# Attention in five rounds of rows a unit, with products in three runs and four rows turned by VectorE

## The chip, the cores and the metric

The kernel runs on one core of a Trainium2 chip. The metric is the device time of one execution in microseconds, as the median of three runs. The engines are TensorE (PE in the profile, PEld for its weight loads), VectorE (DVE), ScalarE (ACT), GpSimd (POOL) and SyncE (SP), which issues most of the DMAs.

## The reference

The input x has shape (8, 1024, 256), float32. One layer norm feeds two branches, and the output is x plus both.

```
xn  = layernorm(x)
qkv = einsum('bse,ehd->bshd', xn, w_qkv)        # 16 heads, q, k, v of 64 each
att = einsum('bshd,hde->bse', attention(q, k, v), w_out)   # causal, logits / sqrt(64), softmax over keys
ffn = top-2-of-8 mixture of experts on xn, capacity 2048 tokens an expert, hidden 1024, relu
out = x + att + ffn
```

## The kernel before, in words

The kernel first does layer norm and routing, then the experts (`experts`), which write their results y to DRAM, and then `attention_and_sum`, the function that the change touches. Products that need precision are made of three matmuls of a high and a low part each (qh and ql, kh and kl, oh and ol, and so on): ScalarE copies a bank of PSUM into the high tile, and VectorE subtracts that from the bank into the low tile.

Attention goes by units: one pair of heads (h = 0, 1) of one batch, UNITS = 8 x 8 = 64. A unit has queries in eight rows of 128 (i = 0 to 7); with the causal mask row i has (i+1) x 128 keys. A unit runs in 16 steps, and each engine's program walks all steps of all units in the same written order, with semaphores between engines; nothing is scheduled at run time. Two steps make one row:

- `scores`: TensorE fills S[0] and S[1] (two banks each) with the row's scores of both heads. It waits until VectorE has read the row before (`negmax`).
- `row_max`: VectorE adds the mask (`late`), writes the scores to a tile pr and gives their minimum, since the scores are negated.
- `softmax`: ScalarE makes the exponential in place with its sum. `reciprocals`: VectorE. The scale by it: GpSimd, in place in pr.
- The scaled row has to be turned, so that keys lie on partitions. For rows 0 to 5 TensorE does it six steps later (`turn_p`, LAG = 6), in blocks of 128 x 128 into the banks T[0] and T[1], chunks of up to four blocks, and `keep` copies each chunk to pT on VectorE (ten chunks a unit) or ScalarE (six). For rows 6 and 7 VectorE transposes squares of 32 x 32 (`square`) into the tile squares, and 16 DMA strips, 12 issued by SP (`place`) and 4 by GpSimd (`place_last`), put the squares in their places of pT. The last unit turns all its rows on TensorE.
- `values`: products of the turned rows with v, by groups of two rows (g = 0 to 3, with 2, 4, 6 and 8 key blocks), into one bank O of 256 columns. `group`: ScalarE copies O to oh, VectorE makes ol.

Between these stand the pieces, each at a step of its own (`STEP_OF`) and in a work bank (`BANK_OF`; two of the three banks are the upper halves of S): p0 to p3 project q and k of the next unit (halves f = 0, 1; p0 and p2 are q, p1 and p3 are k), v0 and v1 project v of the next two units, xn turns a tile of normalised input, and o0 to o3 multiply a group with w_out and add to the residual `res` on VectorE. A piece waits until the piece before it in its bank has been read.

GpSimd also has, at steps of `POOL_AT`: `split_w` and `split_wv` (weights into high and low parts), `choose`, two `fetch`es (gathers of y by indirect DMA), `weigh`, which waits for both fetches, `add` and `total`, which adds the experts' result to `res`. All stand in one queue with the scales.

Of the kernel before, what the change touches and what calls it, by code (L numbers as in the profile page):

```python
# [845 lines left out]
def attention_and_sum(nc, k, x, xn_dram, w_qkv, w_out, pick, y_dram, out, start):  # L846
# [4 lines left out]
    STEPS, LAG, RING = 2 * QT, 6, 8  # L851
# [4 lines left out]
    PART = 8  # L856
    PARTS = [-(-(2 * g + 2) // PART) for g in range(GROUPS)]
    AHEAD = Start.TILES
    VW = 4 * HDIM
    width = lambda s: (s // 2 + 1) * P  # L860
    shift = lambda s: P if width(s) == HALF + P else 0
    slot = lambda n, s: (n * STEPS + s) % RING

    WIDE = STEPS - STEPS // GROUPS
    BL = 32
    QUARTERS = P // BL
    CH = [[b for b in (min(HT, s // 2 + 1), s // 2 + 1 - HT) if b > 0] for s in range(STEPS)]  # L870
    FIRST_CH = [sum(len(x) for x in CH[:s]) for s in range(STEPS + 1)]
    CHUNKS = FIRST_CH[WIDE]
    assert all(FIRST_CH[4 * g] % 2 == 0 for g in range(GROUPS))
    KEPT_BY_ACT = {1, 10, 11, 12, 14, 15} | set(range(CHUNKS, FIRST_CH[STEPS], 2))
    KEPT_BY_DVE = set(range(FIRST_CH[STEPS])) - KEPT_BY_ACT
    in_squares = lambda n, s: s >= WIDE and 0 <= n < UNITS - 1
    by_pe = lambda n, s: 0 <= n < UNITS and not in_squares(n, s)
# [7 lines left out]
    NEXT = 1  # L885
    done_in = lambda n, g: n + (g >= NEXT)
    SHORT = 2 * HT
    BEFORE = ["p0", "p1", "p2", "p3", "v0", "v1"]
    BY_ACT = {"p0", "p1", "p2", "p3", "xn", "v0", "v1"}
    BY_DVE = {"p0", "p1", "p2", "p3", "xn", "o0", "o1", "o2", "o3"}  # L890


    POOL_AT = {'place0': 0, 'place1': 5, 'fetch0': 2, 'fetch1': 5, 'weigh': 6, 'add': 7, 'total': 14, 'split_w': 13, 'split_wv': 10}

    def pieces(n):
        if n < 0:
            return BEFORE
        there = {"p": n + 1 < UNITS, "x": n + AHEAD < TILES, "v": n + 1 < UNITS}

        return [p for p in STEP_OF if there.get(p[0], n < UNITS if p[0] == "o" and int(p[1]) < NEXT else n > 0)]  # L900

    class Pieces:
        def __init__(self, sem_, own):
            self.sem, self.value, at = sem_, {}, 0
            for n in range(-1, UNITS + 1):
                for p in pieces(n):
                    at += p in own
                    self.value[n, p] = at
# [5 lines left out]
    with ExitStack() as c:  # L914
# [6 lines left out]
        qh, ql, kh, kl = (two(lambda i: sb(f"{n}{i}", [P, SEQ], F32R)) for n in ("qh", "ql", "kh", "kl"))  # L921
        vv = two(lambda i: sb(f"vv{i}", [P, QT, VW]))

        pT_even, pT_odd = (sb(f"pT{g}", [P, 2, QT - 2 + 2 * g, GQ]) for g in range(2))
        pT = [[t[:, h] for t in (pT_even, pT_odd)] for h in range(2)]

        wide = pT_odd[:].rearrange("p h k q -> p (h k q)").rearrange("p (a x r) -> p a x r", x=4, a=QUARTERS)

        sq = sb("squares", [P, QUARTERS, 4, QT, BL])
        pr = start.pr + [sb(f"pr{i}", [P, SEQ]) for i in range(len(start.pr), RING)]  # L930
        negm, rsum, rinv = (sb(n, [P, RING]) for n in ("negm", "rsum", "rinv"))
        late = start.late
        oh, ol = (two(lambda i: sb(f"o{n}{i}", [P, GQ], F32R)) for n in "hl")
# [28 lines left out]
        with ExitStack() as pre:  # L962
# [4 lines left out]
            bank = [T[0], T[1], W0, S[0]]  # L967
# [41 lines left out]
        kept = two(lambda i: Count(sem(f"s_kept{i}"), CHUNKS // 2))
        squared = Count(sem("s_squared"), STEPS - WIDE)  # L1010
        placed = Count(sem("s_placed"), 16 * QUARTERS * (QUARTERS - 1))
        last_placed = Count(sem("s_last_placed"), 16 * QUARTERS)
        pv = Count(sem("s_pv"), GROUPS)
        ohi, olo = Count(sem("s_ohi"), GROUPS), Count(sem("s_olo"), GROUPS)
        filled = Pieces(sem("s_filled"), set(BANK_OF))
        act = Pieces(sem("s_act"), BY_ACT)
        dve = Pieces(sem("s_dve"), BY_DVE)

# [12 lines left out]


        lagged = lambda n, s: (n, s - LAG) if s >= LAG else (n - 1, s - LAG + STEPS)
        SQUARE_LAG = 4
        squaring = lambda n, s: (n, s - SQUARE_LAG) if s >= SQUARE_LAG else (n - 1, s - SQUARE_LAG + STEPS)


        AFTER = [13, 14, 19, 27]

        def group_at(n, s):  # L1040

            for d in range(2):
                for g in range(GROUPS):
                    part = s + d * STEPS - AFTER[g]
                    if 0 <= part < PARTS[g] and 0 <= n - d < UNITS:
                        return n - d, g, part
            return None


        OH_LATER, OL_LATER = 0, 0  # L1050
        before = lambda n, s, d: (n, s - d) if s >= d else (n - 1, s - d + STEPS)

        ALL = [(n, s) for n in range(UNITS) for s in range(STEPS)]
        END = [(UNITS, s) for s in range(16)]

        def strip(a, b):

            to, of = slice(b * BL, (b + 1) * BL), slice(a * BL, (a + 1) * BL)
            return wide[to, a].rearrange("p x r -> p (x r)"), sq[of, b].rearrange("p x k i -> p (x k i)")

        @block.sync
        def _(e):
# [8 lines left out]
            def place(n):  # L1071
                e.wait_ge(squared.sem, squared.at(n, STEPS - WIDE))
                e.wait_ge(pv.sem, pv.at(n, GROUPS - 2))
                for a in range(QUARTERS - 1):
                    for b in range(QUARTERS):
                        e.dma_start(*strip(a, b)).then_inc(placed.sem, 16)  # L1076

            def store(b, g):
                e.wait_ge(dve.sem, dve.at(done_in(b * PAIRS + PAIRS - 1, g), f"o{g}"))
                e.dma_start(outv[:, b, 2 * g:2 * g + 2], res[:, 2 * g:2 * g + 2]).then_inc(stored[g].sem, 16)  # L1080
# [8 lines left out]
            e.wait_ge(wlo.sem, wlo.at(0, MC))  # L1089
            load_w(2)  # L1090
            for n in range(UNITS):
                if n + AHEAD < TILES:
# [3 lines left out]
                b, u = n // PAIRS, n % PAIRS  # L1096
                if n == 0:
                    e.wait_ge(s_wolo, 1)
                    for g in range(GROUPS):
                        refill(0, g)  # L1100
                if b > 0 and u == 0:
                    refill(b, 0)
                if b > 0 and u == 1:
                    refill(b, 3)
                if n > 0:
                    place(n - 1)
                if b > 0 and u == 0:
                    store(b - 1, 1)
                    refill(b, 1)
                    store(b - 1, 2)  # L1110
                if n + 3 < UNITS:
                    e.wait_ge(wlo.sem, wlo.at(n + 1, MC))
                    load_w(n + 3)
# [3 lines left out]
                if b > 0 and u == 0:  # L1117
                    store(b - 1, 3)
                    refill(b, 2)
                if u == PAIRS - 1:  # L1120
                    store(b, 0)
            for g in range(NEXT, GROUPS):
# [434 lines left out]
```

## Time and profile before

| | |
|---|---|
| median of three runs | 3163.03 us (3161.75 to 3163.10) |
| span of the profiled execution | 3160.1 us |
| TensorE matmul busy | 3031.1 us, 96% |
| TensorE weight loads busy | 2408.4 us, 76% |
| VectorE busy | 2185.9 us, 69% |
| ScalarE busy | 1711.1 us, 54% |
| GpSimd busy | 1604.3 us, 51% |

The span runs from the first to the last instruction of the profiled execution. Busy time is the time in which an engine has an instruction under way. Matmuls overlap, so TensorE's busy time is not a measure of full speed. The attention takes the last 2250 us or so of the span.

### The profile page before, as it was taken

Reading aid. Unit: us, or ns where it says so; the run is one execution under the profiler, and the core shown is the slowest. Engines: PE = TensorE matmul, PEld = TensorE weight load, DVE = VectorE, ACT = ScalarE, POOL = GpSimd, SP = SyncE. Lnnn points to the kernel's source line nnn. Section 1 sums busy time; section 2 is a strip of 40 time slices with the busy share of each in tenths; the row PEclk is TensorE's granted clock in tenths of the full one; section 3 lists DMA queues with packets and bytes.
Section 4 is the critical chain, followed back from the end, with each engine's and each line's share of the span. In section 5 each row is a group of like instructions: output and inputs, shape, how many; then the busy total and the mean of one; then the engine's idle time right before and its main releaser. Section 6 shows DMA issues by size and latency. Waiting matters only on the chain.

```text
span 3160.1 us, 64379 instructions
## 1 busy us (share of the span) xinstructions
PE 3031.1 (96%) x22707; PEld 2408.4 (76%) x22707; DVE 2185.9 (69%) x5088; ACT 1711.1 (54%) x3866; POOL 1604.3 (51%) x2378
## 2 busy tenths in 40 slices
PE   4699999999989999999999999999999999999998
PEld 3589998999977777777777777777777777777776
DVE  7744443444347778777877787787778877877876
ACT  3454444445446555555555555555555555555554
POOL 3122221222126666666666666666666666666664
PEclk8799999999999999999999999999999999999999
DMA  7112222122113333343333333333442343334222
GB/s 240 49 48 72 77 73 69 47 76 79 51 57 83 95 84 101 80 103 92 87 89 95 101 79 92 102 86 83 101 105 75 86 107 91 82 89 112 71 72 71
DMA packets 204437, 272.64 MB, mean 86 GB/s; under 512 B 61265, under 2 KB 161617, under 8 KB 204129
## 3 DMA queue, kind: packets, MB, share of 16 engines
q1 hardware_dynamic: 179712, 201.94, 23.8%
q0 software_dynamic: 24416, 66.65, 8.0%
q8 instruction: 187, 3.06, 0.4%
q14 instruction: 122, 0.99, 0.1%
HBM read 102.80 MB, written 33.55 MB: 43 GB/s over the span
## 4 chain that ended last, share of the span: by engine, by line
PE 61%; ACT 5%; issue 4%; DVE 1%; SPq 0%; DMA 0%; DVEq 0%; ACTq 0%
PE S L1221 15%; PE O L1258 13%; PE T L1234 10%; PE W L1137 9%; PE S L1137 3%; ACT pr L1296 3%; PE W L1152 3%; PE S L1152 3%; PE W L1172 3%; PE S L1172 2%; ACT pT L1288 1%; PE S L1160 0%; DVE pr L1352 0%; ACT oh L1320 0%; SPq L1076 0%
## 5 line engine op out<-in xcount | busy, mean ns | idle before, releaser
L1296 ACT ACTIVATE pr<-pr,negm 128x128 f32<-128x128 f32 (+7 forms) x1024 | 787.3, 770 | 669.4 <-DVE negm L1352 669.4
L1497 POOL TENSOR_SCALAR pr<-pr,rinv 128x128 f32<-128x128 f32 (+7 forms) x1024 | 755.8, 745 | 424.9 <-DVE rinv L1358 422.5
L1352 DVE CUSTOM_DVE_ANT_0 pr<-S,late 128x128 f32<-128x128 f32 (+7 forms) x1024 | 730.4, 750 | 38.1 <-PE S L1221 22.3
L1258 PE MATMUL O<-pT,vv 128*64 128x256 f32 (+1 forms) x5120 | 556.2, 364 | 3.5 <-DMA pT<-squares 3.1
L1258 PEld LDWEIGHTS O<-pT,vv 128*64 128x64 f32 x5120 | 346.1, 137 | 205.3 <-issue 45.4
L1234 PE MATMUL T<-ident,pr 128*128 128x128 f32 x2718 | 423.4, 281 | 32.5 <-DVE pT L1288 17.8
L832 DVE TENSOR_TENSOR hl<-h,hh 128x512 fp32r<-128x512 f32 x256 | 191.1, 747 | 316.2 <-ACT hh L793 316.0
L1288 DVE COPY pT<-T 128x512 f32<-128x512 f32 (+3 forms) x644 | 305.2, 499 | 142.2 <-PE O L1258 111.9
L1234 PEld LDWEIGHTS T<-ident,pr 128*128 128x128 f32 x2718 | 296.8, 140 | 138.9 <-issue 118.9
L789 ACT ACTIVATE h<-pH,b1c 128x512 f32<-128x512 f32 x256 | 176.1, 688 | 365.6 <-PE pH L719 338.8
L1221 PE MATMUL S<-kh,qh 64*128 64x512 f32 (+2 forms) x1536 | 316.8, 408 | 6.5 <-DVE negm L1352 6.5
L731 PE MATMUL pY<-w2h,hh 128*128 128x256 f32 x1024 | 287.8, 281 | 2.5 <-DVE hl L832 2.5
L731 PE MATMUL pY<-w2l,hh 128*128 128x256 f32 x1024 | 289.1, 282 | 0.0
L731 PE MATMUL pY<-w2h,hl 128*128 128x256 f32 x1024 | 288.0, 281 | 0.0
L1392 DVE STREAM_TRANSPOSE squares<-pr 128x896 f32<-128x896 f32 x252 | 287.7, 1161 | 0.0
L1458 POOL DMA_DIRECT2D pT<-squares x252 | 136.2, 544 | 260.0 <-DVE squares L1392 249.9
L1221 PE MATMUL S<-kh,ql 64*128 64x512 f32 (+2 forms) x1536 | 264.1, 338 | 0.0
L1221 PE MATMUL S<-kl,qh 64*128 64x512 f32 (+2 forms) x1536 | 263.3, 338 | 0.0
L1221 PEld LDWEIGHTS S<-kh,qh 64*128 64x128 f32 x1536 | 144.0, 183 | 126.2 <-issue 65.8
L719 PE MATMUL pH<-xh,w1h 128*128 128x512 f32 x512 | 205.3, 401 | 4.2 <-DVE xl L804 2.6
L719 PE MATMUL pH<-xh,w1l 128*128 128x512 f32 x512 | 201.5, 394 | 0.0
L719 PE MATMUL pH<-xl,w1h 128*128 128x512 f32 x512 | 201.4, 393 | 0.0
(194 smaller groups left out, 6391.3 us busy)
## 6 DMA issues: line engine op xcount, KB each, us to landing
pT<-squares SPq DMA_DIRECT2D x756, 128.0 KB
pT<-squares POOLq DMA_DIRECT2D x252, 128.0 KB, 3.8
y<-yb SPq DMA_DIRECT2D x128, 128.0 KB, 1.7
wr<-in_L_attn_w_qkv SPq DMA_DIRECT2D x128, 128.0 KB, 2.3
x<-in_L_attn_x SPq DMA_DIRECT2D x16, 512.0 KB, 9.7
xn<-xn SPq DMA_DIRECT2D x16, 512.0 KB, 4.5
w1r<-in_L_ffn_w SPq DMA_DIRECT2D x8, 1024.0 KB, 5.0
w2r<-in_L_ffn_w SPq DMA_DIRECT2D x8, 1024.0 KB, 8.0
```

The lines of the kernel that those rows point to most:

```text
L719: ins = e.matmul(pH[hc % 4][:], w[par][:, m, ws], xx[q][:, m, :], start=(n == 0), stop=(n == 3 * MC - 1))
L731: ins = e.matmul(pY[t % 2][:], hs[q][:, hc, ts_], ws[par][:, hc, :], start=(hc == 0 and n == 0), stop=(hc == HC - 1 and n == 2))
L832: e.tensor_tensor(hl[q][:, hc, :], h32[hc % 2][:], hh[q][:, hc, :].bitcast(F32), ALU.subtract).then_inc(hlo.sem, 1)
L1137: ins = e.matmul(W, ws[:, 2 * m + of_k], xs[:, t0:t0 + HT, m, :], start=(i == 0), stop=(i == 3 * MC - 1))
L1221: ins = e.matmul(S[h][:, a:b], t[q][hs, i * P:(i + 1) * P], u[q][hs, a - off:b - off], start=(j == 0), stop=(j == len(terms) - 1))
L1234: ins = e.transpose(T[ch % 2][:, b * P:(b + 1) * P], pr[slot(n, s)][:, kt * P:(kt + 1) * P], k["ident"][:])
L1258: ins = e.matmul(O[hs, a:GQ], vv[n // 2 % 2][:, kt, vs], turned_p, start=(kt == 0), stop=(kt == KT - 1))
L1288: ins = e.activation(dst, src, ACT.Copy) if own is KEPT_BY_ACT else e.tensor_copy(dst, src)
L1296: e.activation(pr[i][:, 0:w], pr[i][:, 0:w], ACT.Exp, bias=negm[:, i:i + 1], scale=-1.0, accum_out=rsum[:, i:i + 1]).then_inc(expd.sem, 1)
L1352: e.tensor_tensor_reduce(pr[i][:, 0:w], S[s % 2][:, off:off + w], late[:, SEQ - w:], 1.0, -MASKED, ALU.add, ALU.min, negm[:, i:i + 1]).the ...
L1392: e.transpose(sq[:, :, x % 2 * 2 + x // 2, 0:KT, :], pr[slot(n, s)][:, 0:KT * P].rearrange("p (k b i) -> p b k i", b=QUARTERS, i=BL)).then ...
L1497: e.tensor_scalar(pr[i][:, 0:width(s)], pr[i][:, 0:width(s)], rinv[:, i:i + 1], 1.0, ALU.mult, ALU.mult).then_inc(scaled.sem, 1)
```

## The change

The unit is rearranged. It has five rounds of four steps, and a round holds one or two rows: (3, 2), (4, 1), (5, 0), (6), (7). The rows of a round stand side by side in S (`OFFSET`), whose four banks now belong to scores alone. TensorE makes all scores of a round, then VectorE takes all minima, and the scores of the next round wait for the last of them. Row 4 is multiplied at 768 columns.

Rows 4 to 7 are turned by VectorE's squares, and groups 2 and 3 each have 16 strips, which SP and GpSimd place at two times of the unit. Rows 0 to 3 are turned by TensorE in six turns (t30 to t11), which are pieces with steps and banks like the others and are all copied by ScalarE. Products come in three runs, groups 0 and 1 together, then 2, then 3, with O and oh, ol of 512 columns, and each group has a pT of its own. q has one buffer (no longer two), and so has the second half of k; for that p2 and p3 project q and k of the unit itself at its steps 0 and 1, and the scores of the round (4, 1) wait for p3's low part. There are three work banks apart from S, and none named T. On VectorE and ScalarE a piece's work stands one step behind the step where TensorE fills it.

```diff
+    ROUNDS = [(3, 2), (4, 1), (5, 0), (6,), (7,)]
+    SUB, RING = 4, 3
+    STEPS = SUB * len(ROUNDS)
+    OFFSET = {3: 0, 2: HALF, 4: 0, 1: HALF + 2 * P, 5: 0, 0: HALF + 2 * P, 6: 0, 7: 0}
+    multiplied_width = {0: 2 * P, 4: 6 * P}
+    SQUARED = [4, 5, 6, 7]
+    TURNS = {"t30": [(3, 0, 0, 4)], "t31": [(3, 1, 0, 4)], "t20": [(2, 0, 0, 3)], "t21": [(2, 1, 0, 3)],
+             "t10": [(1, 0, 0, 2), (0, 0, 0, 1)], "t11": [(1, 1, 0, 2), (0, 1, 0, 1)]}
...
-    STEP_OF = {'v0': 0, 'p0': 2, 'o1': 4, 'o2': 5, 'xn': 5, 'p1': 6, 'v1': 6, 'p2': 7, 'p3': 9, 'o3': 12, 'o0': 14}
-    BANK_OF = {'p0': 2, 'p1': 0, 'p2': 2, 'p3': 2, 'o2': 2, 'xn': 0, 'v0': 2, 'o3': 2, 'v1': 1, 'o0': 2, 'o1': 1}
+    STEP_OF = {"p2": 0, "p3": 1, "o0": 2,
+               "o1": 4, "v0": 5,
+               "t30": 8, "t31": 8, "o2": 9, "t20": 10, "t21": 10,
+               "v1": 12, "p0": 13, "t10": 14, "t11": 14,
+               "p1": 16, "o3": 17, "xn": 18}
+    BANK_OF = {"p2": 0, "p3": 1, "o0": 2,
+               "o1": 0, "v0": 1,
+               "t30": 2, "t31": 0, "o2": 1, "t20": 2, "t21": 0,
+               "v1": 1, "p0": 2, "t10": 0, "t11": 1,
+               "p1": 0, "o3": 2, "xn": 1}
...
-    POOL_AT = {'place0': 0, 'place1': 5, 'fetch0': 2, 'fetch1': 5, 'weigh': 6, 'add': 7, 'total': 14, 'split_w': 13, 'split_wv': 10}
+    RUN_STEP = [(0, 19), (1, 7), (1, 15)]
+    RUN_GROUPS = [(0, 1), (2,), (3,)]
+    POOL_AT = {"choose": 1, "place3_0": 4, "place3_1": 5, "split_w": 6, "fetch0": 8, "fetch1": 9, "weigh": 11, "add": 12,
+               "split_wv": 14, "place2_0": 16, "place2_1": 17, "total": 19}
...
+            def scores(n, r):
+                if r == 0:
                     e.wait_ge(dve.sem, dve.at(n - 1, "p1"))
+                if r == 1:
+                    e.wait_ge(dve.sem, dve.at(n, "p3"))
+                if (n, r) > (0, 0):
+                    e.wait_ge(negmax.sem, negmax.at(n, FIRST[r]))
...
+            def turn_p(n, name):
+                W, unit, at = work_bank(name), min(n, UNITS - 1), 0
+                i, h, _, _ = TURNS[name][-1]
+                e.wait_ge(scaled.sem, scaled.at(unit, PLACE[i, h] + 1))
...
```

The minima on VectorE wait for the room's last reader three rounds before, and for the scores of the whole round:

```diff
+            def row_min(n, j):
+                i, h = ORDER[j]
+                r, off, w, c0 = ROUND_OF[i], OFFSET[i], width(i), column(n, i, h)
...
+                e.wait_ge(score.sem, score.at(n, FIRST[r + 1] - 1 + h))
+                e.tensor_tensor_reduce(room_of(n, i, h)[:, off:off + w], S[h][:, off:off + w], late[:, SEQ - w:], 1.0, -MASKED,
+                                       ALU.add, ALU.min, negm[:, c0:c0 + 1]).then_inc(negmax.sem, 1)
```

The new order of the engines' programs, in turn TensorE, ScalarE, VectorE and GpSimd (whose other work of a step stands behind the step's scale). `names_at` gives the pieces of a step, `run_at` the run of products, `back(n, s, d)` is d steps earlier:

```diff
+                if n < UNITS and s % SUB == 0:
+                    scores(n, s // SUB)
+                for name in names_at(n, s):
+                    work(n, name)
+                if run_at(n, s):
+                    values(*run_at(n, s))
...
+                if run_at(*back(n, s, 1)):
+                    run(*run_at(*back(n, s, 1)))
+                for name in names_at(*back(n, s, 1)):
+                    if by_act(name):
+                        work(back(n, s, 1)[0], name)
+                r, x = s // SUB, s % SUB
+                if n < UNITS and FIRST[r] + x < FIRST[r + 1]:
+                    softmax(n, FIRST[r] + x)
...
+                r, x = s // SUB, s % SUB
+                if run_at(*back(n, s, 1)):
+                    run(*run_at(*back(n, s, 1)))
+                if n < UNITS and x < len(ROUNDS[r]):
                     for h in range(2):
+                        row_min(n, FIRST[r] + 2 * x + h)
...
+                if n < UNITS and 2 <= x < 2 + len(ROUNDS[r]):
+                    reciprocals(n, ROUNDS[r][x - 2])
+                for name in names_at(*back(n, s, 1)):
+                    if by_dve(name):
+                        work(back(n, s, 1)[0], name)
+                m, q = back(n, s, SUB)[0], (r - 1) % len(ROUNDS)
+                if x >= 2 and 0 <= m < UNITS and in_squares(m, ROUNDS[q][0]):
+                    square(m, ROUNDS[q][0], x - 2)
...
+                if x >= 2:
+                    scale(n, FIRST[r] + x - 2)
+                elif m >= 0 and len(ROUNDS[q]) > 1:
+                    scale(m, FIRST[q] + 2 + x)
```

## Rows read from the trace of the kernel before

**Rows 1.** windows, steady stretch: busy us (and instructions) by engine, clock, DMA share, GB/s

```profile
1348.00:1696.00 348.00, 343.17 (x2681) 259.53 (x2680) 274.09 (x670) 200.29 (x491) 217.53 (x335) 1.00 0.36 90
```

**Rows 2.** chain of waits in order of time, one unit: start us, us, what

```profile
2030.07 0.14 issue
...
2031.05 1.42 PE W L1152 x12
...
2035.26 2.53 PE O L1258 x24
...
2047.65 1.48 PE W L1137 x6
...
2049.13 1.25 PE S L1221 x12
...
2051.18 3.39 PE O L1258 x32
...
2056.00 0.59 PE T L1234 x4
...
2058.53 1.59 PE S L1221 x12
```

**Rows 3.** timeline of VectorE (DVE), one unit: start us, us, line, operation

```profile
2026.75 1.22 DVE L1352 CUSTOM_DVE_ANT_0 pr<-S,late 128x1024 f32<-128x1024 f32 x1
...
2031.43 2.09 DVE L1392 STREAM_TRANSPOSE squares<-pr 128x896 f32<-128x896 f32 x2
...
2033.81 0.42 DVE L1352 CUSTOM_DVE_ANT_0 pr<-S,late 128x256 f32<-128x256 f32 x1 [0.24 <-PE S L1221]
...
2046.65 0.69 DVE L1383 TENSOR_TENSOR ql<-W,qh 128x512 fp32r<-128x512 f32 x1 [1.80 <-ACT qh L1311]
...
2047.33 0.80 DVE L1352 CUSTOM_DVE_ANT_0 pr<-S,late 128x640 f32<-128x640 f32 x1
...
2048.06 0.82 DVE L1352 CUSTOM_DVE_ANT_0 pr<-S,late 128x640 f32<-128x640 f32 x1
...
L1288 DVE COPY pT<-T 128x512 f32<-128x512 f32 (+3 forms) x644 | 305.2, 499 | 142.2 <-PE O L1258 111.9
```

**Rows 4.** timeline of GpSimd (POOL): second fetch of y and the weighing behind it

```profile
1035.23 1.02 POOL L1471 DMA_INDIRECT yg<-y,sel  x1 [0.30 <-issue]
...
2044.36 1.02 POOL L1471 DMA_INDIRECT yg<-y,sel  x1 [0.30 <-issue]
...
2049.56 0.93 POOL L1477 TENSOR_SCALAR yg<-yg,sel 128x256 f32<-128x256 f32 x2 [1.34 <-DMA yg<-y,sel]
...
2429.91 1.02 POOL L1471 DMA_INDIRECT yg<-y,sel  x1 [0.30 <-issue]
...
2433.39 0.93 POOL L1477 TENSOR_SCALAR yg<-yg,sel 128x256 f32<-128x256 f32 x2 [1.72 <-DMA yg<-y,sel]
```

**Rows 5.** timeline of ScalarE (ACT): exponentials and a copy

```profile
2028.02 1.14 ACT L1296 ACTIVATE pr<-pr,negm 128x1024 f32<-128x1024 f32 x1
...
2049.01 0.82 ACT L1296 ACTIVATE pr<-pr,negm 128x640 f32<-128x640 f32 x1
...
2049.82 0.57 ACT L1311 ACTIVATE kh<-W 128x512 fp32r<-128x512 f32 x1
```

**Rows 6.** timeline of GpSimd: splits, scales and strip issues of one unit

```profile
2027.77 0.41 POOL L1433 TENSOR_SCALAR wr<-wr 128x256 f32<-128x256 f32 x1
...
2030.52 1.13 POOL L1497 TENSOR_SCALAR pr<-pr,rinv 128x1024 f32<-128x1024 f32 x1
...
2042.98 1.07 POOL L1458 DMA_DIRECT2D pT<-squares  x2
...
2051.83 1.56 POOL L1497 TENSOR_SCALAR pr<-pr,rinv 128x640 f32<-128x640 f32 x2
```

**Rows 7.** timeline of SP, and the page's DMA issues (KB each, us to landing)

```profile
2037.80 9.14 SPq L1076 DMA_DIRECT2D pT<-squares  x12
...
pT<-squares POOLq DMA_DIRECT2D x252, 128.0 KB, 3.8
```

More of the change, by code:

```diff
@@ new lines, in attention_and_sum @@
+    PLACE = {row: j for j, row in enumerate(ORDER)}
+    FIRST = [sum(2 * len(rows) for rows in ROUNDS[:r]) for r in range(len(ROUNDS) + 1)]
+    ROUND_OF = {i: r for r, rows in enumerate(ROUNDS) for i in rows}
+    OFFSET = {3: 0, 2: HALF, 4: 0, 1: HALF + 2 * P, 5: 0, 0: HALF + 2 * P, 6: 0, 7: 0}
+    width = lambda i: (i + 1) * P
+    multiplied_width = {0: 2 * P, 4: 6 * P}
+    room = lambda n, i: (len(ROUNDS) * n + ROUND_OF[i]) % RING
+    column = lambda n, i, h: 4 * room(n, i) + 2 * ROUNDS[ROUND_OF[i]].index(i) + h
@@ new lines, in attention_and_sum, with run_at @@
+    BEFORE = ["p0", "p1", "v0", "v1"]
+    by_act = lambda name: name[0] in "pvx" or (name[0] == "t" and not (len(name) == 4 and name[2] == "1"))
+    by_dve = lambda name: name[0] in "pox" or not by_act(name)
+    RUN_STEP = [(0, 19), (1, 7), (1, 15)]
+    RUN_GROUPS = [(0, 1), (2,), (3,)]
+    RUN_OF = {g: j for j, groups in enumerate(RUN_GROUPS) for g in groups}
+    RUNS = len(RUN_GROUPS)
+    def run_at(n, s):
+        for j, (later, step) in enumerate(RUN_STEP):
+            if s == step and 0 <= n - later < UNITS:
+                return n - later, j
+        return None
@@ L900, in pieces @@
-        return [p for p in STEP_OF if there.get(p[0], n < UNITS if p[0] == "o" and int(p[1]) < NEXT else n > 0)]
+            return [(0, p) for p in BEFORE]
+        there = {"p0": n + 1 < UNITS, "p1": n + 1 < UNITS, "p2": n < UNITS, "p3": n < UNITS, "v0": n + 1 < UNITS,
+                 "v1": n + 1 < UNITS, "xn": n + AHEAD < TILES}
+        own = [(s, p) for p, s in STEP_OF.items() if there.get(p, n > 0 if p[0] == "o" else n < UNITS)]
+        own += [(s, t) for (m, s), turns in END_TURNS.items() if m == n for t in turns]
@@ L902, in attention_and_sum @@
+        return sorted(own, key=lambda at: at[0])
     class Pieces:
@@ L905, in __init__ @@
             for n in range(-1, UNITS + 1):
-                for p in pieces(n):
-                    at += p in own
+                for _, p in pieces(n):
+                    at += own(p)
                     self.value[n, p] = at
@@ L1030, in attention_and_sum, with strip @@
         block = c.enter_context(nc.Block())
[L1033 to L1051, printed above, removed]
+        back = lambda n, s, d: (n, s - d) if s >= d else (n - 1, s - d + STEPS)
         ALL = [(n, s) for n in range(UNITS) for s in range(STEPS)]
-        END = [(UNITS, s) for s in range(16)]
-        def strip(a, b):
+        END = [(UNITS, s) for s in range(STEPS)]
+        names_at = lambda n, s: [p for at, p in pieces(n) if at == s] if n >= 0 else []
+        def strip(g, a, b):
             to, of = slice(b * BL, (b + 1) * BL), slice(a * BL, (a + 1) * BL)
-            return wide[to, a].rearrange("p x r -> p (x r)"), sq[of, b].rearrange("p x k i -> p (x k i)")
+            return wide[g][to, a].rearrange("p x r -> p (x r)"), sq[g][of, b].rearrange("p x k i -> p (x k i)")
         @block.sync
@@ L1118, in _ @@
                     store(b - 1, 3)
[L1119 to L1122, printed above, removed]
+                    refill(b, 3)
+            for g in range(GROUPS):
                 store(BATCH - 1, g)
@@ L1263, in _ @@
-            for name in BEFORE:
+                            vs = slice(n % 2 * P + h * HDIM, n % 2 * P + (h + 1) * HDIM)
+                            turned_p = wide_of(g, h, kt, a // P) if in_squares(n, 2 * g) else pT[g][:, h, kt, a:GQ]
+                            ins = e.matmul(O[hs, o0 + a:o0 + GQ], vv[n // 2 % 2][:, kt, vs], turned_p,
+                                           start=(kt == 0), stop=(kt == KT - 1))
+                ins.then_inc(pv.sem, 1)
+            for _, name in pieces(-1):
```

479 lines of the change are left out of this document (208 added, 271 removed).

## The prediction

> **What bounds the kernel now.** I read the page's totals first, then the windows, then the chain of waits in order of time, then the timelines of the single engines over one unit (one pair of heads of one batch; there are 64). In a 348 us window of the steady part TensorE is busy 343.2 us, VectorE 274, ScalarE 200, GpSimd 218, at a granted clock of 1.00 [rows 1]. A unit lasts 34.80 us: the second fetch of y of 29 units on starts 1009.13 us later [rows 4]. So TensorE is idle about 0.5 us a unit and works 34.3. The chain says the same: matmul pieces follow one another without a gap, scores, products, projections [rows 2]. What TensorE loses, a unit loses; that is true only while the others still fit under it.
>
> **What the change takes from TensorE.** Rows 4 and 5 of both heads were 2x(5+6) = 22 turned blocks. Four blocks take 0.59 us [rows 2], 0.148 each: 3.25 us go. Scores of row 4 grow from 640 to 768 columns. Scores of 768 columns took 1.25 and of 1024 took 1.59 [rows 2], 0.17 per 128 columns, so +0.17. TensorE's work after, from the pieces of rows 2: scores R1 (rows 3, 2) 1.62, R2 (4, 1) 1.80, R3 (5, 0) 1.80, R4 (6) 1.43, R5 (7) 1.59; four projections "p" of 1.5; two "v" of 1.42; four "o" of 0.75 (six matmuls of 256 columns, half of a "v", 0.71, and a little more behind a switch); xn 0.2; 20 blocks 2.96; products run A (groups 0, 1) 2.53, B 2.53, C 3.39. Sum 31.7 us. Group 2 is now read from squares, as group 3 was: 32 such matmuls took 3.39, 24 from plain tiles 2.53, the same 0.106 each, so that costs nothing. Were TensorE still never waiting, a unit would be 31.7.
>
> **What it adds elsewhere.** VectorE loses 10 copies of turned blocks a unit, 0.5 us each [rows 3], and gains four squares of 640 and 768 columns. Two squares of 896 take 2.09 [rows 3], 1.01 each; by columns 0.86 and 0.72, together +3.2. With 27.4 us a unit before [rows 1] it stays under 26, not the bound by its sum. ScalarE takes eight copies where it had six. GpSimd gets four more strip issues, two of which take 1.07 [rows 6], and SP twelve, where twelve take 9.1 [rows 7]: 18.3 of some 35 us, queued behind each other, R5's strips at one time of the unit and group 2's at another, so not the bound.
>
> **What it does to the order.** S now belongs to one round at a time, five rounds a unit, and the fillers between two rounds are few. The sum of shares can't tell whether they cover; I lay one unit out. Time 0 is the start of R5's scores. TensorE goes on 0.14 us after the copy it waited for [rows 2]; I give 0.2 us the other way, from TensorE's last matmul to VectorE's minimum, which waits for it [rows 3]. A minimum takes 0.73 at 640 columns (start to start) and about 0.14 less or more per 128 columns; a subtraction of 512 columns 0.61 and its result is there after 0.69 [rows 3]. An exponential takes 0.81 at 640, start to start, and 1.14 at 1024, about 0.11 per 128 columns, a copy 0.57, of which I count 0.5 where another instruction follows [rows 5]. A scale is 0.78 at 640 on GpSimd, 0.11 per 128 columns; the split of weights from 2027.77 to 2030.52 is 2.75 [rows 6].
>
> *First wait, R1 to R2.* TensorE: R5 scores to 1.6, p1 3.1, o3 3.85, xn 4.05, run A 6.55, R1 scores 8.2, p2 9.7, p3 11.2, o0 11.95, free. VectorE: minima of row 7 1.8 to 4.1; ScalarE's exponentials with p1's copy between them end at 5.95; behind the reciprocal that waits for them stand o3's addition, two squares of row 6 (2.0), xn's low part, run A's low part (0.6): 9.65. Only now come R1's four minima, though their scores were there at 8.4: 11.8. Then p2's low part, and p3's, which waits for ScalarE, where p3's copy stands behind two exponentials and p2's: 12.9; done 13.6. R2's scores wait for that by program: they start at 13.7. TensorE waits 1.75.
>
> *R2 to R3*: TensorE: scores 15.5, o1 16.25, v0 17.65, run B 20.2. VectorE: square of row 7 (1.17), a reciprocal, o0's addition (0.6), the other square: 16.6, also the moment from which group 3's strips can be issued; four minima (0.73 and 0.3, twice): 18.8, before TensorE is through. No wait.
>
> *Second wait, inside R3.* Scores end 22.0; t30, t31, o2 to 23.95. t20 wants t30's bank, and ScalarE copies t30 only after the exponential of row 5, whose minimum ends 1.15 after the scores (23.2): exponential 24.15, copy over at 24.7, t20 at 24.85, t21 likewise behind t31, done 25.75. TensorE has lost 0.85.
>
> *Third wait, inside R4.* TensorE: scores 27.2, v1 28.6, p0 30.1, t10, t11 to 31.0. t11 wants the bank of v1, whose copy stands behind row 6's exponential; VectorE is late at row 6's minimum: R3's minima are over at 24.4, but ScalarE's queue is exponential of 5, copies t30 and t31, exponential of 5 (26.2), one of 0, copies t20 and t21, one of 0 (27.9). So VectorE has the reciprocal of row 5 at 26.3, o2's addition and a square of row 4 to 27.6, the reciprocal of row 0 at 28.0, the other square to 28.7. Then minimum 29.8, exponential 30.85, v1's copy 31.45. t11 also wants row 0 scaled by GpSimd. That queue, from the squares of row 7 at 16.7: two strips 1.1, a scale 0.55, two strips 1.1, 0.76, split 2.75, 0.76, 0.45, fetch 1.1, 0.45, second fetch at 25.9. "weigh" stands before row 0's scale and waits for that fetch. In the usual unit it is there 5.2 us after its start, behind SP's strips; in a unit whose strips had just been issued, 3.5 [rows 4]. The new order has the fetch behind the last strip (16.7 + 9.1 = 25.8), so I take 3.5: 29.4, weigh 0.9, scale 0.35, add 0.73, scale 0.35: 31.8. t11 31.9 to 32.3, run C to 35.7, R5 again. Wait 1.3. Strips of group 3 have landed at 25.8 + 3.8 [rows 7] = 29.6, in time.
>
> 31.7 + 1.75 + 0.85 + 1.3 gives 35.6, the layout 35.7: 0.9 us more than 34.80. TensorE's removed work turned into three waits that are larger. Over 62 units +56 us. The first and last unit I take as before; the end may go either way by some 6 us.
>
> The Trainium skill (Perfetto Trace Analysis, Optimizing Scalar/DVE Operations) advises that where ScalarE and VectorE are not saturated but cause bubbles, cutting their instructions up may finish work sooner; this change groups them instead. By the shares alone a unit would be 31.7 us, by that rule bubbles should appear; no row of before shows it.
>
> The profiled execution spans 3160.1 us and the runs' median is 3163.0, so 2.9 us lie around it. 3163.0 + 56 = **3219 us**.
>
> **Rivals.**
> *A, GpSimd's fetch late.* If it takes the usual 5.2 us, it is there at 31.1: weigh to 32.0, scale 32.35, add 33.1, scale 33.45, t11 to 34.0, run C to 37.4, a period of 37.4 and +161 us, 3324. For it: this is the common case in the trace. Against: the strips are over earlier here. Chance 0.15.
> *B, faster: the first wait is shorter.* Place: VectorE's work between row 7's reciprocal and R1's first minimum. The layout has R1's minima 1.25 us behind their scores. The exact order of ends there is mine, and if VectorE is on time, with ScalarE's copies of p2 and p3 no later than TensorE fills them, R2 starts at 12.4 and all behind moves up: 34.4, 3163 - 25 = 3138. It decides from 0.9 us on. For it: 3.1 us of TensorE's work is really gone, so the waits must eat all of it. Against: the chain is a program order of seven instructions whose durations the trace shows. Chance 0.2.
> *C, all covered*: 31.7, 62 x -3.1, 2971. The second wait alone speaks against it, since the copy stands behind an exponential by program order. Chance 0.03.
> *D, about as before*: waits add up to 3.1. Chance 0.06.
> *Forecast*, three waits of 3.5 to 4.7 together, 3180 to 3260: 0.56.
>
> Within 0.2% (6 us) is no change that a measurement can tell. Faster: B and C, 0.23; same: D, 0.06; slower: the rest, 0.71. The forecast's own range is 3180 to 3260. The range of 8 in 10 reaches from 3120, most of B, to 3325, A.
>
> **What would show it.** A unit of 35 to 36.5 us between fetches; TensorE busy about 31.7 of it, some 89%; three gaps a unit: before R2's scores, released by VectorE's low part of k (1.7); before t20 and t21, by ScalarE's copies (0.9 together); before t10 or t11, by ScalarE's copy of v1 or GpSimd's scale (1.3). VectorE 26 us, GpSimd 24. Group 2's matmuls 0.106 us apart. Wrong would be: R1's minima start right behind their scores (B), weigh waits long behind the fetch and t11 for the scale (A), or run C waits for strips, which the layout excludes by 2.7 us.

## The result, and the profile after

The changed kernel takes 3289.95 us (median of four runs, 3280.67 to 3299.98) against 3162.39 before; the ratio is 1.0403, 95% interval 1.0382 to 1.0424. The forecast was 3219, with 3180 to 3260 as its own range and 3120 to 3325 as the range of 8 in 10. The way was right, but the loss of 127 us is more than twice the 56 that were forecast. It lies in the wide range only because that reached up to rival A, whose reason (a gather of 5.2 us) did not come about. Per unit the loss is 2.03 us and not 0.9: the second fetches of units lie 36.83 us apart on average over 60 units, against 34.80 [rows 4].

TensorE's totals on the page of the changed kernel:

```profile
PE 2915.4 (89%) x21321; PEld 2329.7 (71%) x21321; DVE 2120.5 (65%) x4640; ACT 1702.1 (52%) x3934; POOL 1740.3 (53%) x2631
```

The windows of the changed kernel, first the stretch of [rows 1], then two of 5 us (columns as there):

```profile
1348.00:1696.00 348.00, 304.88 (x2315) 232.16 (x2313) 248.12 (x570) 186.02 (x470) 226.87 (x358) 0.96 0.52 126
2010.00:2015.00 5.00, 5.00 (x35) 2.98 (x34) 1.80 (x3) 0.55 (x2) 3.76 (x6) 0.71 0.36 98
2030.00:2035.00 5.00, 5.00 (x32) 4.36 (x32) 4.39 (x12) 2.54 (x6) 3.56 (x7) 0.67 0.48 119
```

TensorE is busy 304.9 of 348 us (343.2 before), VectorE 248 (274.1 before), both less than before, and no engine is full. New is the clock: 0.96 over the stretch, and 0.71 and 0.67 in the two short windows, that is, 1.2 GHz for more than half of them and 2.4 GHz for the rest. Before it was 1.00 over the stretch. Both short windows come behind gaps of TensorE:

```profile
2008.79 0.52 PE L1183 MATMUL W<-ident,pr 128*128 128x128 f32 x3 [1.94 <-POOL pr L1429]
...
2028.67 0.50 PE L1225 MATMUL S<-khf,qh 64*128 64x512 f32 x2 [1.95 <-DVE kls L1383]
```

The chain of waits of the changed kernel, one unit from the low part of run A's products (start us, us, what):

```profile
2024.11 0.65 DVE ol L1399
2024.76 0.60 DVE pr L1349
2025.41 0.82 ACT pr L1287 x2
2026.22 0.48 ACT qh L1307
2026.70 0.70 ACT pr L1287 x2
2027.41 0.49 ACT khs L1307
2027.93 0.69 DVE kls L1383
2028.62 1.15 DVE squares L1392
...
2029.81 0.59 DVE res L1375
2030.40 1.16 DVE squares L1392
...
2031.85 1.05 POOL pT L1460 x2
...
2036.67 1.44 POOL wl L1441 x2
...
2039.52 1.06 POOL yg L1473
...
2041.30 4.39 DMA yg<-y,sel
...
2045.77 0.94 POOL yg L1479 x2
2046.71 0.35 POOL pr L1429
2047.06 0.70 POOL yg L1484
2047.75 0.36 POOL pr L1429
...
2048.25 0.52 PE W L1183 x3
2048.77 3.39 PE O L1257 x32
2052.16 1.64 PE S L1225 x11
```

In this stretch hardly any of it is TensorE up to t11. L1399 is ol, L1349 a minimum, L1287 an exponential, L1307 the copies of p2 and p3, L1383 p3's low part, L1392 the squares of row 7 with o0's addition (L1375) between them, L1460 GpSimd's strips, L1441 the split, L1473 the fetches, L1479 weigh, L1429 scales, L1484 add, L1183 t11, L1257 run C, L1225 the scores of round R5. It is the layout's path in its order. Against the start of the R5 scores before (2015.18 in the chain) the second fetch stands at 26.1, the layout had 25.9; the fetch takes 4.4 and the layout 3.5; from weigh to t11 it is 2.5, as laid out. Not every unit goes this way: of 49 units between 1200 and 3000 us the chain goes through the fetch in 34, and in 12 more it comes to t11 over ScalarE's copy of v1 instead.

TensorE's timeline in the changed kernel, with the idle time ahead of a row in brackets, and run C behind the last:

```profile
2047.20 0.52 PE L1183 MATMUL W<-ident,pr 128*128 128x128 f32 x3 [0.74 <-POOL pr L1429]
2048.25 0.52 PE L1183 MATMUL W<-ident,pr 128*128 128x128 f32 x3 [0.53 <-POOL pr L1429]
...
2065.66 0.49 PE L1225 MATMUL S<-khf,qh 64*128 64x512 f32 x2 [1.96 <-DVE kls L1383]
...
2076.48 1.03 PE L1183 MATMUL W<-ident,pr 128*128 128x128 f32 x6 [0.96 <-ACT pT L1277]
...
2083.49 0.52 PE L1183 MATMUL W<-ident,pr 128*128 128x128 f32 x3 [1.53 <-POOL pr L1429]
2084.54 0.87 PE L1183 MATMUL W<-ident,pr 128*128 128x128 f32 x3 [0.53 <-ACT qh L1307]
2085.34 4.73 PE L1257 MATMUL O<-pT,vv 128*64 128x256 f32 x32
```

The waits of 1900 us (51.5 units), in total, times and longest:

```profile
PE S L1225 <- DVE kls L1383: 99.8, 51, 2.0
...
PE W L1183 <- POOL pr L1429: 65.1, 72, 2.2
...
PE W L1183 <- ACT pT L1277: 50.4, 52, 1.0
...
PE W L1183 <- ACT vv L1298: 11.9, 16, 1.1
```

The three waits stand where they were forecast, the first 1.96 us (forecast 1.75), the second 0.96 (0.85), the third in two parts, 1.5 us a unit on average (1.3). The row at 2084.54 names the copy to qh, which t11 doesn't wait for by program; it ended about when row 0's second scale did, and that scale is what t11 waits for.

Before, the 32 matmuls of run C took 3.46 us as one piece of the timeline in all 58 units read:

```profile
2051.11 3.46 PE L1258 MATMUL O<-pT,vv 128*64 128x256 f32 x32
```

Here they take 4.73. Over 54 units of the changed kernel they average 3.98, in 19 of them more than 3.6, the longest 6.09: 0.52 us a unit that no step of the prediction had. In those 19 units t10 and t11 had waited 1.7 to 2.7 us together (2.28 on average), in the other 35 from 0.5 to 1.8 (1.05).

GpSimd's second fetch and the weighing behind it in the changed kernel answer to [rows 4]:

```profile
2041.30 1.04 POOL L1473 DMA_INDIRECT yg<-y,sel  x1 [0.19 <-issue]
...
2045.77 0.94 POOL L1479 TENSOR_SCALAR yg<-yg,sel 128x256 f32<-128x256 f32 x2 [1.33 <-DMA yg<-y,sel]
```

From start to weigh it is 4.47 us in this unit and 3.66 on average over 61 units (2.9 to 4.8). Before it was 5.2 on average over 64 units (3.5 to 6.1).

### The profile page after: what moved, and what is told of

It is laid out like the page before. It is cut to its first block, busy times and chain, and to the rows that moved or that the text cites. A ratio compares the mean times of both kernels' runs of the same rounds, so it can differ in the third digit from the quotient of the medians.

```text
span 3285.6 us, 61637 instructions
## 1 busy us (share of the span) xinstructions
PE 2915.4 (89%) x21321; PEld 2329.7 (71%) x21321; DVE 2120.5 (65%) x4640; ACT 1702.1 (52%) x3934; POOL 1740.3 (53%) x2631
## 4 chain that ended last, share of the span: by engine, by line
PE 18%; POOL 14%; DVE 14%; ACT 11%; issue 10%; DMA 5%; DVEq 0%; ACTq 0%; POOLq 0%
PE O L1257 9%; ACT pr L1287 8%; DVE squares L1392 6%; PE S L1225 6%; POOL pr L1429 5%; DMA yg<-y,sel 5%; POOL pT L1460 3%; DVE pr L1349 2%; DVE res L1375 2%; POOL wl L1441 2%; POOL yg L1473 1%; DVE kls L1383 1%; PE W L1183 1%; DVE ol L1399 1%; POOL yg L1479 1%
## 5 line engine op out<-in xcount | busy, mean ns | idle before, releaser
L1287 ACT ACTIVATE pr<-pr,negm 128x512 f32<-128x512 f32 (+7 forms) x1024 | 786.3, 770 | 839.8 <-DVE negm L1349 839.8
L1429 POOL TENSOR_SCALAR pr<-pr,rinv 128x512 f32<-128x512 f32 (+7 forms) x1024 | 762.0, 750 | 619.4 <-DVE rinv L1355 605.5
L1349 DVE CUSTOM_DVE_ANT_0 pr<-S,late 128x512 f32<-128x512 f32 (+7 forms) x1024 | 715.1, 749 | 108.8 <-PE S L1225 108.8
L1257 PE MATMUL O<-pT,vv 128*64 128x256 f32 (+1 forms) x5120 | 570.7, 376 | 0.0
L1392 DVE STREAM_TRANSPOSE squares<-pr 128x640 f32<-128x640 f32 x504 | 512.3, 1027 | 0.0
L1257 PEld LDWEIGHTS O<-pT,vv 128*64 128x64 f32 x5120 | 359.9, 142 | 196.3 <-issue 47.8
L1183 PE MATMUL W<-ident,pr 128*128 128x128 f32 x1332 | 214.3, 288 | 159.8 <-POOL pr L1429 75.1
L1225 PE MATMUL S<-khf,qh 64*128 64x512 f32 (+2 forms) x1024 | 221.1, 427 | 125.5 <-DVE kls L1383 125.5
L1460 POOL DMA_DIRECT2D pT<-squares x504 | 263.2, 529 | 113.3 <-DVE squares L1392 110.9
L1183 PEld LDWEIGHTS W<-ident,pr 128*128 128x128 f32 x1332 | 142.6, 142 | 231.0 <-ACT pT L1277 92.5
L1225 PEld LDWEIGHTS S<-khf,qh 64*128 64x128 f32 x1024 | 98.8, 188 | 185.2 <-DVE kls L1383 138.9
L1138 PE MATMUL W<-xnh,wh 128*128 128x512 f32 x512 | 216.7, 423 | 1.2 <-PEq L987 1.2
L1399 DVE TENSOR_TENSOR ol<-O,oh 128x256 fp32r<-128x256 f32 (+1 forms) x192 | 96.1, 501 | 166.0 <-ACT oh L1318 162.5
L1138 PE MATMUL W<-xnh,wl 128*128 128x512 f32 x512 | 203.0, 396 | 0.0
```

The source lines that it names most:

```text
L1138: ins = e.matmul(W, ws[:, 2 * m + of_k], xs[:, t0:t0 + HT, m, :], start=(i == 0), stop=(i == 3 * MC - 1))
L1183: ins = e.transpose(W[:, at * P:(at + 1) * P], room_of(unit, i, h)[:, cols], k["ident"][:])
L1225: ins = e.matmul(S[h][:, off + f * HALF:off + f * HALF + cols], t[hs, i * P:(i + 1) * P], u[f][n % 2][hs, 0:cols], start=(j == 0), stop=(j ...
L1257: ins = e.matmul(O[hs, o0 + a:o0 + GQ], vv[n // 2 % 2][:, kt, vs], turned_p, start=(kt == 0), stop=(kt == KT - 1))
L1287: e.activation(p, p, ACT.Exp, bias=negm[:, c0:c0 + 1], scale=-1.0, accum_out=rsum[:, c0:c0 + 1]).then_inc(expd.sem, 1)
L1349: e.tensor_tensor_reduce(room_of(n, i, h)[:, off:off + w], S[h][:, off:off + w], late[:, SEQ - w:], 1.0, -MASKED, ALU.add, ALU.min, negm[: ...
```

## The experiments

All ratios are to the kernel before, whose median stayed between 3161.8 and 3163.5.

| run | us | ratio (95%) | unit us | clock of the profile |
|---|---|---|---|---|
| changed | 3289.95 | 1.0403 (1.0382 to 1.0424) | 36.83 | 0.964 |
| e1_fetch_early | 3190.96 | 1.0095 (1.0078 to 1.0112) | 35.24 | 0.978 |
| e2_square6_early | 3269.61 | 1.0337 (1.0320 to 1.0355) | 36.64 | 0.970 |
| e3_copies_first | 3312.36 | 1.0476 (1.0459 to 1.0494) | 37.20 | 0.960 |
| e4_fill_gaps | 3259.59 | 1.0310 (1.0293 to 1.0328) | 36.35 | 0.990 |
| f1_fetch_square | 3123.79 | 0.9876 (0.9859 to 0.9892) | 34.24 | 0.988 |
| f2_fetch_v1 | 3126.18 | 0.9885 (0.9869 to 0.9902) | 34.17 | 0.987 |
| f3_all | 3035.64 | 0.9601 (0.9585 to 0.9617) | 32.72 | 0.988 |
| f4_fetch_fill | 3159.68 | 0.9990 (0.9981 to 1.0000) | 34.77 | 0.989 |
| g1_weigh_late | 3192.77 | 1.0096 (1.0079 to 1.0113) | 35.29 | 0.979 |
| g2_all_weigh_late | 2998.09 | 0.9481 (0.9466 to 0.9497) | 32.16 | 0.988 |

The clock of the last column is the mean granted clock of the whole span; 0.990 is the value of the kernel before too.

**e1, the fetches early.**

```diff
-    POOL_AT = {"choose": 1, "place3_0": 4, "place3_1": 5, "split_w": 6, "fetch0": 8, "fetch1": 9, "weigh": 11, "add": 12,
+    POOL_AT = {"choose": 1, "place3_0": 4, "place3_1": 5, "split_w": 6, "fetch0": 2, "fetch1": 3, "weigh": 11, "add": 12,
```

> The changed kernel with GpSimd's two fetches of y at steps 2 and 3 (they were at 8 and 9), ahead of the strips, so that weigh at step 11 waits for nothing. Theory 1 (the third wait is GpSimd's queue with the fetch in it, as the chain of waits of the changed kernel shows): weigh follows the scales of row 5 at once, row 0 is scaled 1 to 3 us sooner, and t11 then waits only for ScalarE's copy of v1, about 0.7 us sooner in a unit with a late fetch and 0 to 0.3 in others; with the clock dropping less often behind the shorter gap, a unit of 36.2 to 36.5 instead of 36.83, 3250 to 3270 us. Rival (ScalarE's copy of v1 alone sets t11, the fetch is hidden beside it): within 10 us of the changed kernel, 3280 to 3295.

99 us came back, 1.6 us a unit, far more than the 20 to 40 that were expected. TensorE's gaps in one unit of e1:

```profile
2014.46 0.50 PE L1225 MATMUL S<-khf,qh 64*128 64x512 f32 x2 [1.96 <-DVE kls L1383]
...
2026.80 1.03 PE L1183 MATMUL W<-ident,pr 128*128 128x128 f32 x6 [0.97 <-ACT pT L1277]
...
2033.31 0.55 PE L1183 MATMUL W<-ident,pr 128*128 128x128 f32 x3 [0.71 <-ACT vv L1298]
```

The third wait is now a single one of 0.71, released by ScalarE's copy of v1 (L1298). Two things make the gain larger. Run C takes 3.46 us in all 57 units read, with a wait of 0.7 us ahead of it instead of 1.5 on average: that is 0.52 of the 1.6 us. And what is left was mis-sized: these gaps and a unit of 34.79 without low clock (2033.86 to 2068.65 in the chain, the starts of run C) leave 31.15 us of work for TensorE, where the prediction had summed 31.7. So TensorE's own path was half a us further ahead of GpSimd's than the layout said, and the fetch was worth more. The clock still falls in e1, behind the first gap, which adds the rest to the mean of 35.24.

**g1, weigh late instead.** The fetches stay at 8 and 9.

```diff
-    POOL_AT = {"choose": 1, "place3_0": 4, "place3_1": 5, "split_w": 6, "fetch0": 8, "fetch1": 9, "weigh": 11, "add": 12,
+    POOL_AT = {"choose": 1, "place3_0": 4, "place3_1": 5, "split_w": 6, "fetch0": 8, "fetch1": 9, "weigh": 13, "add": 15,
```

> The changed kernel with both fetches where they are, at steps 8 and 9, and weigh and add moved from steps 11 and 12 to 13 and 15, behind both scales of row 0, so that nothing that TensorE waits for stands behind the fetch's landing. Landing theory (the third wait is the time from the second fetch's start to its landing, 3 to 4.8 us): t11 no longer waits for GpSimd, a unit is as long as with the fetches early, 35.0 to 35.3 us, 3180 to 3200 us. Rival (early fetches helped by taking 2.1 us of issuing out of GpSimd's queue between the squares of row 7 and row 0's scale, and moving weigh doesn't): only a part of the 99 us comes, 3225 to 3270.

It is as fast as e1 within the intervals. It was the landing that stood ahead of row 0's scales, not the time to issue the fetches.

**e2, row 6's squares a step earlier.**

```diff
-                if x >= 2 and 0 <= m < UNITS and in_squares(m, ROUNDS[q][0]):
-                    square(m, ROUNDS[q][0], x - 2)
+                first = 1 if r == 4 else 2
+                if first <= x < first + 2 and 0 <= m < UNITS and in_squares(m, ROUNDS[q][0]):
+                    square(m, ROUNDS[q][0], x - first)
```

> The changed kernel with the two squares of row 6 one step earlier on VectorE (steps 17 and 18 for 18 and 19), the first of them ahead of row 7's reciprocal, in time in which VectorE waits for ScalarE. Theory 1 (VectorE's backlog ahead of the round (3, 2) sets the first wait): the minima of that round start up to 0.6 us sooner and TensorE's gap before the scores of (4, 1) shrinks from 1.96 to 1.3 to 1.5, 0.5 us a unit, 3255 to 3265 us. Rival (the chain from ScalarE, exponentials and copies of p2 and p3, sets that gap whatever VectorE does): gap and time as in the changed kernel, 3280 to 3295.

The gap shrank as expected, 1.4 us for 1.96, and 0.54 us a unit should have followed; 0.2 did, and the time lies between the two forecasts. The second fetch does start 0.55 us sooner behind the R5 scores (25.68 for 26.24, means of 49 and 48 units). But run C averages 4.33 us over 55 units here, 0.35 more than in the changed kernel: it stands in low clock more often (30 units, not 19), as the waits of t10 and t11 grow from 1.5 to 2.0 us.

**e3, ScalarE copies t30 and t31 ahead of the exponential of row 5.**

```diff
                 for name in names_at(*back(n, s, 1)):
-                    if by_act(name):
+                    if by_act(name) and name not in ("t30", "t31"):
                         work(back(n, s, 1)[0], name)
+                for name in names_at(n, s):
+                    if name in ("t30", "t31"):
+                        work(n, name)
```

> The changed kernel with ScalarE's copies of t30 and t31 ahead of the first exponential of row 5. Theory 1 (the second wait is the order on ScalarE): TensorE's gap before t20 goes from 0.96 to under 0.2, and 0.3 to 0.9 us a unit come back, since what follows on VectorE and ScalarE starts no later; 3235 to 3270 us. Rival (TensorE's gap only moves to the next wait, which GpSimd's queue sets from the squares of row 7 on, independent of when the scores of row 6 are made): the gap before t20 goes, that before t10 grows by as much, and the time stays at 3280 to 3295.

The rival was right on the place and neither on the time: the kernel is 22 us slower. The gap before t20 is gone. Half of it is now a wait of 0.44 us ahead of v1, for VectorE's addition of o2, and one unit of e3 shows where the rest went:

```profile
2052.18 0.52 PE L1183 MATMUL W<-ident,pr 128*128 128x128 f32 x3 [2.55 <-POOL pr L1432]
2053.23 0.52 PE L1183 MATMUL W<-ident,pr 128*128 128x128 f32 x3 [0.53 <-POOL pr L1432]
2053.68 5.11 PE L1257 MATMUL O<-pT,vv 128*64 128x256 f32 x32
```

It is now a longer gap just ahead of run C, 2.55 us before t10 in this unit; on average t10 waits 1.76 us, against 0.92 in the changed kernel. Run C averages 4.55 us over 54 units, slow in 37 of them.

**e4, the gaps filled with useless matmuls.** p0 is made twice and o0 three times, into the same bank with the same values.

```diff
+                for again in range(2 if name == "p0" and n >= 0 else 1):
+                    i = 0
+                    for m in range(MC):
+                        for ws, xs in ((wh, xnh), (wh, xnl), (wl, xnh)):
...
-                for t in range(2):
+                for t in [0, 1] * (3 if g == 0 else 1):
```

> The changed kernel with more work: TensorE makes o0 three times and p0 twice in each unit, into the same bank with the same result, 2.9 us a unit of matmuls, placed in the gaps ahead of the scores of (4, 1) and ahead of t10. Theory 1 (a part of the loss is TensorE's clock, whose granted value is 0.964 on average and about 0.7 in 5 us windows behind the gaps, where 32 matmuls of run C take 4.5 us for 3.4): with the gaps filled the granted clock is above 0.99 and the kernel gets faster although it does more, a unit 0.8 to 1.3 us shorter, 3205 to 3240 us. Rival (the gaps, not the clock, set the time; the low clock falls where TensorE waits anyway): the same time or slower, 3285 to 3330.

The windows of e4, the same stretch:

```profile
1348.00:1696.00 348.00, 324.98 (x2526) 252.71 (x2524) 252.71 (x580) 192.01 (x488) 234.92 (x371) 1.00 0.53 131
```

2.9 us more of matmuls a unit, and 30 us less time. The clock is 1.00, run C takes 3.46 us in all 55 units read. The chain's other parts stay: from the R5 scores to the second fetch 26.2 us and from there to weigh 3.8, in both kernels. The unit is 0.48 us shorter, which is run C's 0.52. The gain is below what was expected. In all, the low clock costs TensorE 1.4 us a unit in the changed kernel (32.6 busy for 31.15), but the other slow matmuls (o and v behind the first gap, and runs A and B) lie for the most part where TensorE is ahead of the chain, and only shorten its waits.

**f4, the same test where TensorE's own path sets the time:** e1, and o0 three times.

> The fetches early (e1), and o0 made three times into the same bank with the same result, 1.4 us more of matmuls a unit in the gap of 1.96 ahead of the scores of (4, 1). Clock theory: the granted clock goes from 0.985 to 1.00, since in e1 it falls behind that gap in a part of the units, and the time falls by 20 to 30 us to 3160 to 3172 although TensorE does more. Rival (only the gap itself costs): 3188 to 3200.

TensorE's gaps in a unit of f4:

```profile
2033.37 0.50 PE L1225 MATMUL S<-khf,qh 64*128 64x512 f32 x2 [0.55 <-DVE kls L1383]
...
2044.19 1.03 PE L1183 MATMUL W<-ident,pr 128*128 128x128 f32 x6 [0.97 <-ACT pT L1277]
...
2050.69 0.55 PE L1183 MATMUL W<-ident,pr 128*128 128x128 f32 x3 [0.71 <-ACT vv L1298]
```

The unit goes from 35.24 to 34.77, and is 34.8 in e1 wherever the clock had not fallen. 31 us are gained by 1.4 us of added work a unit, most of it in a gap that was 1.96 and is 0.55.

**f1, f2 and f3, the waits taken away by order.** f1 is e1 and e2. f2 is e1 with v1 in the place of t30 and t31 in e3's edit. f3 is e1, e2 and e3's edit for t30, t31 and v1, and

```diff
-                if run_at(*back(n, s, 1)):
+                if s and run_at(*back(n, s, 1)):
                     run(*run_at(*back(n, s, 1)))
                 if n < UNITS and x < len(ROUNDS[r]):
                     for h in range(2):
                         row_min(n, FIRST[r] + 2 * x + h)
+                if s == 0 and run_at(*back(n, s, 1)):
+                    run(*run_at(*back(n, s, 1)))
```

> The fetches early (e1) and the two squares of row 6 a step earlier (e2) together. Theory 2 (with the fetch early the unit is a plain sum of TensorE's work and three gaps, so a gap that gets shorter comes back in full): TensorE's gap before the scores of (4, 1) goes from 1.96 to 1.42 as in e2, 0.54 us a unit, 33 us in all, from 3191 to 3150 to 3165. Rival (the 20 us of e2 alone were all that this edit is worth, the rest returns in the gap before t11): 3170 to 3185.

> The fetches early (e1), and ScalarE copies v1 ahead of the first exponential of row 6, in time in which it waits for that row's minimum. Theory 2 (with the fetch early the third wait is the order on ScalarE): the gap of 0.71 us before t11 falls below 0.2 and the time by 30 to 45 us, 3145 to 3165. Rival (row 0's scale, behind weigh and add on GpSimd, stands as close behind): t11 then waits for GpSimd, and 5 to 15 us are gained at most, 3175 to 3190.

> Five edits of order together: fetches early, squares of row 6 early, run A's low part on VectorE behind the first two minima of the round (3, 2) instead of ahead of them, and on ScalarE the copies of t30, t31 and v1 ahead of the exponential that they stood behind. Theory 2 (all of the loss is the order of the queues, the new arrangement itself is good): the gaps go from 1.96, 0.97 and 0.71 to about 0.8, 0.1 and 0, and the granted clock stays at 1.00, a unit of 32.6 to 33.3 us, 3030 to 3075 us, below the kernel before. Rival (VectorE, with 26 us of work and waits for ScalarE between, becomes the bound as soon as TensorE's gaps close): a unit of 34 or more, 3120 to 3160.

f1 and f2 came out faster than expected. f1 gained 67 us over e1 where its gap gives 33, f2 65 where its gap gives 44. TensorE's gaps in a unit of f1:

```profile
2014.79 0.50 PE L1225 MATMUL S<-khf,qh 64*128 64x512 f32 x2 [1.42 <-DVE kls L1383]
...
2025.63 1.03 PE L1183 MATMUL W<-ident,pr 128*128 128x128 f32 x6 [0.96 <-ACT pT L1277]
...
2032.14 0.55 PE L1183 MATMUL W<-ident,pr 128*128 128x128 f32 x3 [0.71 <-ACT vv L1298]
```

The rest is clock again: of 400 windows of 5 us from 1000 to 3000 us, 21 have a clock under 0.9 in e1, none in f1 and 2 in f2 (51 in the changed kernel, none before). f3 came out within its forecast. Its gaps are 1.00, 0.44 and 0.28:

```profile
2000.52 0.50 PE L1225 MATMUL S<-khf,qh 64*128 64x512 f32 x2 [1.00 <-DVE kls L1386]
...
2013.05 0.39 PE L1153 MATMUL W<-wvh,xnh 128*128 128x256 f32 x1 [0.44 <-DVE res L1378]
...
2016.73 0.52 PE L1183 MATMUL W<-ident,pr 128*128 128x128 f32 x3 [0.28 <-POOL pr L1435]
```

**g2, f3 with weigh and add late.**

> The five edits of order together (f3) and weigh and add at steps 13 and 15. In f3 the chain of waits still goes through GpSimd's scales, weigh (0.9 us) and add (0.7 us) to t11, which waits 0.3 us for them. If GpSimd's queue is what is left, t11 goes up to 0.3 us sooner and a unit falls from 32.7 to about 32.4, 3010 to 3025 us. Rival (another wait, VectorE's addition ahead of v1 or the low part of k, is as long): 3028 to 3042.

The windows of g2, the same stretch:

```profile
1348.00:1696.00 348.00, 330.74 (x2644) 257.55 (x2644) 281.87 (x643) 212.57 (x538) 259.61 (x408) 1.00 0.55 143
```

A unit takes 32.16 us, half a us less than in f3, and the gain is more than expected. In f3 the chain of waits ran through GpSimd's instructions for 14.9 us of each unit, in g2 for 0.3; so what GpSimd had set was more than the last 0.3 us before t11. TensorE is busy 330.7 of 348 us in g2, VectorE 282. It is the fastest of all versions, 5.2% below the kernel before.

## Why the prediction came out as it did

- *TensorE loses 22 turned blocks and gains 128 columns of scores; products from squares cost nothing.* Right in kind, and the difference was right in size too: 34.3 - 3.25 + 0.17 is 31.2, and 31.15 was measured. But the prediction went on with its sum of pieces, 31.7, half a us more. The largest part of that is in the scores: it gave the three rounds of two rows 1.62, 1.80 and 1.80 us, and at full clock they take 1.42, 1.61 and 1.60 (f1). By itself that error makes a forecast too high where TensorE sets the time; here it hid a part of the third wait's error.
- *First wait, 1.75 us, VectorE's backlog and then ScalarE's copies ahead of p3's low part.* Right: 1.96, in the order laid out. e2 and f3 took it down to 1.4 and 1.0 by moving what stood in that backlog.
- *Second wait, 0.85, ScalarE's exponential ahead of the copy of t30.* Right: 0.96; e3 removed it, and waits further on took its place.
- *Third wait, 1.3, GpSimd's fetch with weigh ahead of row 0's scale, and ScalarE's copy of v1 close behind.* Right in place and in queue; e1 and g1 show both parts. The size was too small. On average over 49 units of e4, where the clock is full, it is 26.2 us from the R5 scores to the second fetch (layout 25.9), 3.8 from there to weigh ("so I take 3.5"), 2.5 to t11 (2.5), 0.5 to run C (0.4) and 3.4 for run C (3.4). That is the unit of 36.35, against the layout's 35.7. In the terms of the sum the third wait was 36.35 - 31.15 - 1.96 - 0.96 = 2.3 us at full clock and not 1.3, of which half a us only makes up for the work that was summed too high. In the changed kernel itself it shows as 1.5, because TensorE comes to it later with its slower matmuls.
- *What failed is two terms of the sum.* One is the third wait's size, just told: 0.6 us a unit against the layout, some 39 of the 71 us that were missed. The other is a term that the text put at nothing without an argument. [rows 1] had a granted clock of 1.00, and every duration of TensorE was carried over at it, run C's 3.39 too. With gaps in TensorE's work the clock fell to its lower level behind them, and run C, which follows the third wait, took 0.52 us more on average. That is 32 us of the 71, and e4 gave 30 of them back with the waits of the other engines left as they were.
- Rival A (fetch late) had the right queue but not the landing: 3.66 and not 5.2. That 3290 lies nearer to its 3324 than to 3219 is chance. That the gather would be there sooner behind strips that are already issued fits what was measured. Rival B wanted 0.9 us less of the first wait alone. f1 came below the kernel before with 0.54 us less of it and an early fetch; the first wait alone (e2) gave 20 us.
- *Bubbles.* The Trainium skill (Perfetto Trace Analysis, Optimizing Scalar/DVE Operations) says that cutting instructions up may help where ScalarE and VectorE cause bubbles without being saturated; the prediction turned that round into a forecast that grouping makes bubbles, which the section does not say. The bubbles came, but f3 and g2 keep every round and every instruction at its size and lose most of them by order alone: TensorE is idle 4.5 us a unit in the changed kernel, 1.9 in f3 and 1.6 in g2. Whether smaller instructions would do it too, no run here shows.

What stays open: how far a gap must go before the clock falls. In f1, with 1.4, 0.96 and 0.71 us a unit, it was under 0.9 in none of 400 windows; in e1, with 1.96 for the first, it fell in about every third unit. It isn't the longest gap alone: f2 keeps the 1.96 and the 0.97, without the 0.71, and has 2 such windows where e1 has 21.

## What to carry to other kernels

A sum of busy shares can say that an arrangement has room, not that its order uses it; here the same work took 36.8 us a unit in one order and 32.2 in another. Where a sum of pieces and a difference from what was measured disagree, as 31.7 and 31.2 did here, find out why before going on. Lay one unit out by hand, find the instruction in each in-order queue that waits for something slow (a gather, a result two engines away), and put behind it only what nobody is waiting for. And where TensorE gets gaps, price its work behind them at the lower clock as well.

## What the runs showed of the hardware

Useless matmuls made a kernel faster: 2.9 us of them a unit took 30 us off (e4), 1.4 us took 31 off (f4), each with the granted clock at 1.00 in the steady stretch (0.96 in the changed kernel, 0.985 in e1). And removing a wait can cost: in e3 the wait before t20 went and the one before t10 grew from 0.92 to 1.76 us on average (3.6 at most), and the 32 matmuls of run C behind it went from 3.98 to 4.55. Weigh could start 2.9 to 4.8 us after the start of a gather of y that was issued behind the last strip. In the kernel before, where SP was still issuing strips, it was 5.2 in the unit of [rows 4]; no run here separates the strips from the other traffic.
